# Attention with P times V of key blocks 1, 2 and 3 issued as one group in place of two

## The chip, the cores and the metric

The kernel runs on one core of one Trainium2 chip. The metric is the device time of one execution in microseconds (us); lower is better.

## The reference

One layer of a pre-norm transformer on x of 4 batches, 512 rows and 1024 columns, all in fp32. The attention has 32 query heads of 32 columns, which share one key and one value head. The second half multiplies by a weight of 6-bit codes.

```
q = (hidden_states @ Wq).reshape(b, s, NUM_HEADS, HEAD_DIM)
kv = hidden_states @ Wkv
k, v = (kv[..., :HEAD_DIM], kv[..., HEAD_DIM:])
scores = jnp.einsum('bqhd,bkd->bhqk', q, k) * scale
...
scores = jnp.where(causal[None, None], scores + bias[None], -jnp.inf)
attn = jax.nn.softmax(scores, axis=-1)
out = jnp.einsum('bhqk,bkd->bqhd', attn, v).reshape(b, s, h)
return out @ Wo
...
x = x + _L0_attn_ref(_layernorm(x, axis=-1), L0_attn_Wq, L0_attn_Wkv, L0_attn_Wo)
x = x + _L0_ffn_ref(_layernorm(x, axis=-1), L0_ffn_qweight, L0_ffn_weight_scale, L0_ffn_weight_zero_point, L0_ffn_bias)
```

The change touches only the product of attn and v.

## The kernel before

Four stages follow one another: `project` (layer norm, q, k and v), `attend` (the attention), `split_wo`, and `finish` (output projection and the second half). Only `attend` is changed.

`attend` makes 32 **steps**, one for each batch and group of four heads. Each engine has a program of its own, in the fixed order in which the code issues it; semaphores tie them together. The scores are computed twice. First with queries on the partitions (`score`, tile `p_s`), to find each query's maximum: VectorE (DVE) reduces each block with `maximum`, one column of `mx` for each. Then with keys on the partitions (`score_t`, tile `p_st`), where the maximum enters as two more rows of the contraction; ScalarE (ACT) takes the exponential of it into `pt`, GpSimd (POOL) cuts the diagonal and adds parts for the row totals, and TensorE (PE) multiplies `pt` with V (`values`, tile `p_o`) and with a column of ones (`totals`, tile `p_sum`).

PE's program for step s is a ring of 12 **positions**, 0 to 11. At each stands one `score_t` (at position 5 the transpose `turn_max` in its place), then one or two `score` for a later step (two at positions 0, 3, 6 and 9), and at some positions a group for step s-1, by the tables `VALUES_AT` and `TOTALS_AT`. These say: before, key block 0 at position 1, block 1 at position 4, blocks 2 and 3 at position 6, and the totals at position 9. The scores of one step are named here s0 to s15 as PE issues them: s0 and s1 at position 0, s2 at 1, s3 at 2, s4 and s5 at 3, s6 at 4, s7 at 5, s8 and s9 at 6, s10 at 7, s11 at 8. Their widths are 128, 256, 384 and 512 columns in turn. The maxima on DVE are max0 to max15 in the same order.

The matmuls of `score` and `score_t` are fp32r with 128 stationary columns. Those of `values` and `totals` are fp32 with 32 stationary columns, one for each head in its own quarter of the array (`tile_position`), and four of them, one per head, run at once. `turn_max` is an fp32 transpose of the full array. The trace calls all of these "f32".

How a maximum gets to its use: s3 completes the 16 blocks of the next step, max3 writes the last of them into `mx`, `turn_max` at position 5 waits for it and transposes `mx` into a bank of `p_st`. ACT rounds it (`max_high`, tile `mh`), DVE computes the rest (`max_low`, tile `ml`), and SyncE sends both by DMA into `qst`, where `score_t` at position 0 of the next step reads them. `max_low` is written in DVE's program behind max9 (`if i == 9`). The bank is one of three that `score_t` uses in turn, so `score_t` at position 8, the next user of it, waits for `ml_done` (`free_bank`).

`maximum` waits for the score it reduces; for a block of 128 columns it waits for the next score too (`n + 2 if qb == 0`), since the two share a bank. So max8 waits for s8 and s9.

Of the kernel before, what the change touches and what calls it, by code (L numbers as in the profile page):

```python
# [413 lines left out]
def attend(nc, wo, qh_d, ql_d, ext_d, inv_d, keep, ot, wo_raw):  # L414
# [3 lines left out]
    with ExitStack() as ctx:  # L418
# [84 lines left out]
        def _(pe):  # L503
# [34 lines left out]
            def values(s, kb):  # L538
                b = s // GROUPS
                if kb == 0:  # L540
                    at_least(pe, o_taken, s)
                pe.wait_ge(cut_done, 4 * s + kb + 1)
                for h in range(4):
                    last = pe.matmul(p_o[32 * h:32 * h + 32, kb * P:S], vst[:, TPB * b + kb, :],  # L544
                                     pt[s % 2][:, h, PT_AT[kb]:PT_AT[kb] + KB_LEN[kb]], start=(kb == 0), stop=(kb == 3),
                                     tile_position=(0, 32 * h), skip_group_check=True)
                if kb == 3:
                    last.then_inc(v_done, 1)
# [11 lines left out]
                if part == 1:  # L560
                    last.then_inc(pv_done, 1)

            VALUES_AT = {1: (0,), 4: (1,), 6: (2, 3)}
            TOTALS_AT = {9: (0, 1)}

            def step(s):
                n = 4 * (4 * s + AHEAD)
                for at in range(RING):
# [8 lines left out]
                    if s > 0:  # L577
                        for kb in VALUES_AT.get(at, ()):
                            values(s - 1, kb)
# [483 lines left out]
```

## Time and profile before

| | us |
|---|---|
| median of 3 runs | 979.53 |
| lowest and highest | 978.84 and 981.4 |
| the profiled execution | 978.43 |
| its span, first to last instruction | 976.7 |

The 32 steps of `attend` take some 300 of the 976.7 us, from about 280 to 600. The profile's timeline gives for each instruction its start and its duration in us, and in square brackets how long its engine sat idle before it and which engine ended that. A matmul's duration is modelled and overlaps with that of the next; what a matmul costs is the distance from its start to the next start. PE is the matmul, PEld is the weight load. Rows of `values` are counted x8 for four matmuls of one width, x16 for eight.

### The profile page before, as it was taken

What the parts mean: (1) busy time and instruction counts of PE and PEld (TensorE: products, weight loads), DVE (VectorE), ACT (ScalarE), POOL (GpSimd) and SP (SyncE); (2) the same over time, 40 slices, a digit from 0 to 9 for tenths busy, and PEclk for the clock granted to TensorE, in tenths of its full rate; (3) what the DMA queues carried; (4) which work ended last, traced back from release to release, by engine and by line L of the source; (5) the groups of instructions that cost most, each with busy time, mean ns of one, the idle gap of its engine ahead of it and who ended that gap; (6) DMA issues with size and microseconds to landing.
All of it is one profiled execution on the core that took longest, in us unless ns stands there. A gap on an engine that the chain in (4) does not pass through costs nothing. (4 is left out here: it accounts for less than half of the span.)

```text
span 976.7 us, 13682 instructions
## 1 busy us (share of the span) xinstructions
PE 871.9 (89%) x4912; PEld 633.4 (65%) x4912; DVE 528.9 (54%) x1466; ACT 335.0 (34%) x639; POOL 404.6 (41%) x270
## 2 busy tenths in 40 slices
PE   3689999999488999999999996069999999999996
PEld 2578888888354555555555552047888778887885
DVE  6454352611185777877787781413545564556444
ACT  3222121221034666666666664321111211121111
POOL 1100000000015888888888887134533453335410
PEclk9899999999857999999999998578999999999999
DMA  4533545434574343443334310460242224222311
GB/s 145 193 116 117 187 137 176 147 103 124 135 238 86 80 91 82 90 93 89 84 87 95 86 36 12 147 207 22 73 119 68 65 65 120 74 65 65 104 47 43
DMA packets 63675, 100.52 MB, mean 103 GB/s; under 512 B 6132, under 2 KB 31732, under 8 KB 63544
## 3 DMA queue, kind: packets, MB, share of 16 engines
q1 hardware_dynamic: 61944, 93.62, 35.1%
q0 software_dynamic: 1664, 6.03, 2.0%
q8 instruction: 39, 0.64, 0.3%
q14 instruction: 28, 0.23, 0.1%
HBM read 68.56 MB, written 30.54 MB: 101 GB/s over the span
## 5 line engine op out<-in xcount | busy, mean ns | idle before, releaser
L675 DVE CUSTOM_DVE_ANT_0 spill<-p_s,mask 128x128 bf16<-128x128 f32 (+3 forms) x512 | 224.3, 486 | 89.2 <-PE p_s L512 87.3
L608 ACT ACTIVATE pt<-p_st 128x512 f32<-128x512 f32 (+1 forms) x352 | 179.7, 562 | 98.6 <-PE p_st L535 92.8
L512 PE MATMUL p_s<-kst,qst 98*128 98x128 f32 (+3 forms) x512 | 154.9, 349 | 13.1 <-DMA qst<-ext_d 13.0
L535 PE MATMUL p_st<-qst,kst 100*128 100x512 f32 (+1 forms) x352 | 147.7, 424 | 7.3 <-DMA qst<-ml 6.6
L512 PEld LDWEIGHTS p_s<-kst,qst 98*128 98x128 f32 x512 | 104.0, 206 | 27.6 <-issue 13.5
L828 PE MATMUL p_wo<-woh,osh 128*128 128x512 f32 x256 | 82.7, 405 | 39.4 <-POOL osl L908 37.9
L647 POOL TENSOR_TENSOR pt<-pt 128x1536 f32<-128x1536 f32 x32 | 111.7, 3490 | 2.7
L640 POOL TENSOR_SCALAR_AFFINE_SELECT pt<-pt 128x512 f32<-128x512 f32 x128 | 80.3, 642 | 76.6 <-ACT pt L608 76.6
L908 POOL TENSOR_TENSOR osl<-ot,osh 128x1024 fp32r<-128x1024 f32 x16 | 38.5, 2404 | 171.6 <-ACT osh L868 171.6
L217 PE MATMUL p_q<-xth,wqh 128*128 128x512 f32 x256 | 103.5, 404 | 4.4 <-DVE wql L392 4.4
L535 PEld LDWEIGHTS p_st<-qst,kst 100*128 100x128 f32 x352 | 68.4, 195 | 60.1 <-ACT pt L608 27.1
L217 PE MATMUL p_q<-xtl,wqh 128*128 128x512 f32 x256 | 101.2, 395 | 0.0
L217 PE MATMUL p_q<-xth,wql 128*128 128x512 f32 x256 | 101.1, 395 | 0.0
L949 DVE TENSOR_TENSOR xr<-xr,p_wo 128x1024 f32<-128x1024 f32 x16 | 19.5, 1221 | 137.5 <-PE p_wo L828 137.5
L544 PE MATMUL p_o<-pt,vst 128*32 128x512 f32 (+3 forms) x1024 | 89.6, 445 | 1.7 <-POOL pt L640 1.7
L656 POOL MEMSET mx<- 128x128 f32 x2 | 0.3, 199 | 215.6 <-POOLq L68 215.6
L873 ACT ACTIVATE mv<-mv,eps 128x1 f32<-128x1 f32 x16 | 4.7, 295 | 229.3 <-DVE mv L955 229.3
L838 PE MATMUL p_ff<-wi,yth 128*128 128x512 f32 x256 | 79.8, 393 | 2.9 <-DVE ytl L966 2.9
L828 PEld LDWEIGHTS p_wo<-woh,osh 128*128 128x128 f32 x256 | 48.1, 193 | 52.8 <-POOL osl L908 41.7
L828 PE MATMUL p_wo<-wol,osh 128*128 128x512 f32 x256 | 80.4, 396 | 0.0
L828 PE MATMUL p_wo<-woh,osl 128*128 128x512 f32 x256 | 80.2, 395 | 0.0
L838 PE MATMUL p_ff<-wi,ytl 128*128 128x512 f32 x256 | 79.8, 393 | 0.0
(99 smaller groups left out, 1264.4 us busy)
## 6 DMA issues: line engine op xcount, KB each, us to landing
qst<-qh_d SPq DMA_DIRECT2D x64, 256.0 KB
xin<-in_x_dram SPq DMA_DIRECT2D x16, 512.0 KB, 3.9
qh_d<-qh SPq DMA_DIRECT2D x32, 256.0 KB, 2.6
ql_d<-ql SPq DMA_DIRECT2D x32, 256.0 KB, 3.2
qst<-ql_d SPq DMA_DIRECT2D x32, 256.0 KB
inv_b<-inv_d SPq DMA_DIRECT2D x64, 128.0 KB, 4.8
xr<-in_x_dram SPq DMA_DIRECT2D x16, 512.0 KB, 4.2
out_dram<-ot SPq DMA_DIRECT2D x16, 512.0 KB, 5.2
```

What stands on the lines that cost most here:

```text
L217: last = pe.matmul(out, w[:, c, cols], xt[:, bass.ds(at + c, 1), :].rearrange("p a s -> p (a s)"), start=(c == 0 and k == 0), stop=(c == C ...
L512: pe.matmul(scores_of(n), qst[s % 4][0:R_MAX, j, qb * P:(qb + 1) * P], kst[0:R_MAX, b * S:b * S + keys], start=True, stop=True).then_inc(s ...
L535: pe.matmul(p_st[:, place(k) % 3, 0:heads * KB_LEN[kb]], kst[0:R_END, b * S + kb * P:b * S + (kb + 1) * P], qst[s % 4][0:R_END, j:j + head ...
L544: last = pe.matmul(p_o[32 * h:32 * h + 32, kb * P:S], vst[:, TPB * b + kb, :], pt[s % 2][:, h, PT_AT[kb]:PT_AT[kb] + KB_LEN[kb]], start=(k ...
L608: act.activation(pt[s % 2][:, j:j + heads, PT_AT[kb]:PT_AT[kb] + KB_LEN[kb]], p_st[:, place(k) % 3, 0:heads * KB_LEN[kb]].rearrange("p (j ...
L640: pool.affine_select(out=own, in_=own, compare_op=ALU.is_ge, fill=0.0, base=0, pattern=[[0, 4], [1, P]], channel_multiplier=-1).then_inc(c ...
L647: pool.tensor_tensor(x[:, :, ADD_AT:ADD_AT + 3 * P], x[:, :, PT_AT[0] + P:PT_AT[0] + S], x[:, :, PT_AT[1]:PT_AT[1] + 3 * P], ALU.add).then ...
L675: dve.tensor_tensor_reduce(spill[:, SPILL_AT[qb]:SPILL_AT[qb] + keys], scores_of(n), mask[:, S - keys:S], 1.0, LOWEST, ALU.add, ALU.max, m ...
L828: last = pe.matmul(p_wo[:, n, :], a[:, c, :], w[:, c, n * S:(n + 1) * S], start=(c == 0 and k == 0), stop=(c == CK - 1 and k == 2))
L838: last = pe.matmul(p_ff[:, n, :], a[:, c, :], wi[:, c, n * S:(n + 1) * S], start=(c == 0 and a is yth), stop=(c == CK - 1 and a is ytl))
L908: pool.tensor_tensor(osl[:, :, :].rearrange("p c q -> p (c q)"), o_tile(t), osh[:, :, :].rearrange("p c q -> p (c q)"), ALU.subtract).then ...
L949: dve.tensor_tensor(xt, xt, flat(p_wo[:, :, :]), ALU.add).then_inc(x2_done, 1)
```

## The change

The table of positions is changed. Block 1 moves from position 4 to position 5, behind the transpose and s7; blocks 2 and 3 move from position 6 to position 5, ahead of that position's end. The three then stand behind one another. Nothing is added or taken out.

```
-            VALUES_AT = {1: (0,), 4: (1,), 6: (2, 3)}
+            VALUES_AT = {1: (0,), 5: (1, 2, 3)}
```

The order of PE's program changes, in 31 of the 32 steps (in step 0 there is no earlier step to multiply). The programs of DVE, ACT, POOL and SyncE are the same before and after. The last step's own products stand behind the ring and are not changed.

PE before, from position 4 to the `score_t` of position 8 (`p_st<-qst,kst` is `score_t`, `p_s<-kst,qst` is `score`, `p_st<-ident,mx` is the transpose, `32x384` and the like are `values`):

```order
L535 MATMUL p_st<-qst,kst 128x384
L512 MATMUL p_s<-kst,qst 128x384
L544 MATMUL p_o<-pt,vst 32x384 x4
L527 MATMUL p_st<-ident,mx 128x128
L512 MATMUL p_s<-kst,qst 128x512
L535 MATMUL p_st<-qst,kst 128x384
L512 MATMUL p_s<-kst,qst 128x128
L512 MATMUL p_s<-kst,qst 128x256
L544 MATMUL p_o<-pt,vst 32x256 x4
L544 MATMUL p_o<-pt,vst 32x128 x4
L535 MATMUL p_st<-qst,kst 128x384
L512 MATMUL p_s<-kst,qst 128x384
```

PE after, the same place:

```order
L535 MATMUL p_st<-qst,kst 128x384
L512 MATMUL p_s<-kst,qst 128x384
L527 MATMUL p_st<-ident,mx 128x128
L512 MATMUL p_s<-kst,qst 128x512
L544 MATMUL p_o<-pt,vst 32x384 x4
L544 MATMUL p_o<-pt,vst 32x256 x4
L544 MATMUL p_o<-pt,vst 32x128 x4
L535 MATMUL p_st<-qst,kst 128x384
L512 MATMUL p_s<-kst,qst 128x128
L512 MATMUL p_s<-kst,qst 128x256
L535 MATMUL p_st<-qst,kst 128x384
L512 MATMUL p_s<-kst,qst 128x384
```

Two things moved: the transpose has no `values` ahead of it any more, and s8 and s9 (128 and 256 columns) now stand behind all of blocks 1, 2 and 3, where they stood ahead of blocks 2 and 3. The next instruction behind each excerpt is the `score_t` of position 8.

## Rows read from the trace of the kernel before

**Rows 1.** Head of the page: the span and the busy time of each engine.
```profile
span 976.7 us, 13682 instructions
PE 871.9 (89%) x4912; PEld 633.4 (65%) x4912; DVE 528.9 (54%) x1466; ACT 335.0 (34%) x639; POOL 404.6 (41%) x270
```

**Rows 2.** Busy time by stretch: start and end, length, then each engine, granted clock last.
```profile
320.75:330.50 9.75, 9.75 (x78) 5.63 (x77) 7.22 (x36) 6.33 (x14) 8.25 (x7) 1.00 0.38 86
330.50:505.72 175.22, 175.22 (x1369) 101.17 (x1369) 135.57 (x604) 114.80 (x237) 148.50 (x109) 1.00 0.39 87
620.00:976.00 356.00, 316.33 (x1408) 258.88 (x1408) 167.25 (x179) 58.28 (x97) 131.58 (x53) 0.95 0.30 88
```

**Rows 3.** Timeline of PE, an inner step, from block 0 to position 8.
```profile
320.75 1.06 PE L544 MATMUL p_o<-pt,vst 128*32 128x512 f32 x8
321.75 0.50 PE L535 MATMUL p_st<-qst,kst 100*128 100x512 f32 x1
322.09 0.40 PE L512 MATMUL p_s<-kst,qst 98*128 98x512 f32 x1
322.32 0.40 PE L535 MATMUL p_st<-qst,kst 100*128 100x512 f32 x1
...
322.98 0.33 PE L512 MATMUL p_s<-kst,qst 98*128 98x384 f32 x1
323.25 0.85 PE L544 MATMUL p_o<-pt,vst 128*32 128x384 f32 x8
324.03 0.33 PE L527 MATMUL p_st<-ident,mx 128*128 128x128 f32 x1
324.12 0.48 PE L512 MATMUL p_s<-kst,qst 98*128 98x512 f32 x1
324.43 0.34 PE L535 MATMUL p_st<-qst,kst 100*128 100x384 f32 x1
324.61 0.39 PE L512 MATMUL p_s<-kst,qst 98*128 98x128 f32 x2
324.93 0.86 PE L544 MATMUL p_o<-pt,vst 128*32 128x256 f32 x16
325.72 0.44 PE L535 MATMUL p_st<-qst,kst 100*128 100x384 f32 x1
326.00 0.33 PE L512 MATMUL p_s<-kst,qst 98*128 98x384 f32 x1
326.24 0.44 PE L535 MATMUL p_st<-qst,kst 100*128 100x384 f32 x1
```

**Rows 4.** Timeline of the same step: max3, POOL's addition, ml, position 8.
```profile
322.63 0.69 DVE L675 CUSTOM_DVE_ANT_0 spill<-p_s,mask 128x512 bf16<-128x512 f32 x1 [0.82 <-PE p_s L512]
...
322.90 2.38 POOL L653 TENSOR_TENSOR pt<-pt 128x1024 f32<-128x1024 f32 x1
...
323.25 0.08 DVE L675 DVE_READ_ACCUMULATOR2_ANT mx<- 128x1 f32 x1
...
325.92 0.27 DVE L682 SCALAR_TENSOR_TENSOR ml<-p_st,mh 16x128 fp32r<-16x128 f32 x1
...
326.24 0.19 PEld L535 LDWEIGHTS p_st<-qst,kst 100*128 100x128 f32 x1 [0.22 <-DVE ml L682]
```

**Rows 5.** Timeline of step 0, which has no values groups, positions 6 to 8.
```profile
285.73 0.63 PE L512 MATMUL p_s<-kst,qst 98*128 98x128 f32 x2
...
286.50 0.29 DVE L675 CUSTOM_DVE_ANT_0 spill<-p_s,mask 128x128 bf16<-128x128 f32 x1
...
286.72 0.42 DVE L675 CUSTOM_DVE_ANT_0 spill<-p_s,mask 128x256 bf16<-128x256 f32 x1
...
287.06 0.27 DVE L682 SCALAR_TENSOR_TENSOR ml<-p_st,mh 16x128 fp32r<-16x128 f32 x1
...
287.39 0.69 PE L535 MATMUL p_st<-qst,kst 100*128 100x384 f32 x1 [0.40 <-DVE ml L682]
```

**Rows 6.** Timeline of POOL near the end of the stage, step 30.
```profile
589.80 3.48 POOL L647 TENSOR_TENSOR pt<-pt 128x1536 f32<-128x1536 f32 x1
```

## The prediction

> **What bounds the kernel now.** I read the head of the page first, then the busy time by stretch, then the timeline of one inner step. The head shows PE busy for 89% of the span, the next engine 54% [rows 1]. The stretches show that inner steps are alike: 320.75 to 330.50 is one step, and 330.50 to 505.72 is 18 steps in 175.22 us, 9.73 us each. In both PE is busy all the time at a granted clock of 1.00 (2.4 GHz), while DVE has 7.2 of 9.75 us, ACT 6.3 and POOL 8.25 [rows 2]. So the step lasts as long as PE needs for its list, plus whatever PE waits. The timeline shows how near such waits are. At position 8, the weight load was released by ml on DVE: ml starts at 325.92, lasts 0.27, ends at 326.19, and PE goes on at 326.24 [rows 3, 4]. s10, of 384 columns, starts at 326.00; the `score_t` of 384 columns at 324.43 is followed by the next start after 0.18, so PE was ready for position 8 at 326.18 [rows 3]. It lost 0.06 us. This chain (s9, max9, ml, position 8) has no slack before the change; the total shares of busy time don't tell this.
>
> **What a group costs beside its columns.** Block 0, 512 columns, takes 321.75 - 320.75 = 1.00 us; block 1, 384 columns, 324.03 - 323.25 = 0.78; blocks 2 and 3, together 384 columns, 325.72 - 324.93 = 0.79 [rows 3]. So 128 columns cost 0.22, blocks behind one another add nothing, and a group has a fixed part of about 1.00 - 4 x 0.22 = 0.12 to 0.15 us. Further, the last score ahead of a group takes longer (322.98 to 323.25 is 0.27 against 0.18, so 0.08 to 0.09 for the entry), and the first `score_t` behind one also (325.72 to 326.00 is 0.28 against 0.18, 0.10 for a weight load that isn't hidden) [rows 3]. One group fewer saves some 0.15 + 0.08 + 0.10 = 0.33 us a step. But before, the transpose rode directly behind block 1, in place of that `score_t`: T to s7 is 0.09 and s7 to the next is 0.31, against 0.23 for a 512-column score such as 322.09 to 322.32 [rows 3]. It needs these 0.40 us wherever it stands.
>
> The Trainium skill (TensorEngine Tiling (Array Packing), Key Properties) says that a change of tiling mode drains TensorE. The rows' 0.12 to 0.15 of fixed cost agrees with that. Going by the rule alone, one switch to quarter-array tiles and back is dropped in each step, nothing is added, and the kernel gets faster; that is rival A below.
>
> **The new step, instruction by instruction.** I lay the changed list on the clock of the inner step, which runs unchanged up to s6 at 322.98.
> - PE is ready for the transpose at 322.98 + 0.18 = 323.16. The transpose needs max3: it starts at 322.63, its last read of the accumulator is 323.25 + 0.08 = 323.33 [rows 4], and a release takes PE about 0.05 (ml end 326.19, PE 326.24). So the transpose starts at 323.39: a new wait of 0.23. Before, block 1 covered it, and nothing showed.
> - s7 at 323.39 + 0.09 = 323.48. Behind it the group can start after 0.31 + 0.08: 323.87. No row shows a transpose, one score and a group in a row; 0.31 is what s7 takes before, and the least is 0.23, so the start lies between 323.71 and 323.87. I take the later, as 0.31 is from the same pair.
> - The group has 768 columns: 1.00 + 2 x 0.22 = 1.44, so position 6 starts at 325.31.
> - Position 6: its `score_t` pays the unhidden load, 0.28, so s8 and s9 start at 325.59, 0.98 us later than the 324.61 of before [rows 3].
> - PE would then be ready for position 8 after 0.24 + 0.18 + 0.18 (a pair of 384 columns without a group behind it, a `score_t` of 384, s10): 326.19. That is 0.05 ahead of the 326.24 of before. So far the change is worth about nothing: the transpose's wait and its own mode change eat the saving.
> - But max8 waits for s8 and s9, and ml stands behind max9. Duration of the pair 0.39, end 325.98. DVE starts 0.14 behind a score's end (322.09 + 0.40 = 322.49, max3 at 322.63). max8 to max9 takes 0.22, max9 to ml 0.34, ml 0.27, release 0.06 [rows 3 to 5]. Sum 325.98 + 0.14 + 0.22 + 0.34 + 0.27 + 0.06 = 327.01.
> - Position 8 starts at 327.01 in place of 326.24: **+0.77 us** a step, of which PE waits 0.82 for ml.
>
> Step 0 shows this very order, since it has no groups: s8 and s9 at 285.73, max8 at 286.50, ml at 287.06, position 8 at 287.39 with a wait put down to ml [rows 5]. From the pair's end (285.73 + 0.63 = 286.36) that is 1.03 us; my sum above has the same 1.03.
>
> **What follows position 8.** From there all four engines keep their distance to PE. ml ends just ahead of position 8 before and after, so its DMA to `qst`, needed at position 0 of the next step, has the same time. POOL's cut of block 1 follows the exponential of position 8, and has 1.5 us of idle in a step (9.75 - 8.25, [rows 2]); it shifts with PE. Blocks 2 and 3 are wanted 0.4 us earlier (324.93 before; 323.87 plus 0.66 for block 1 is 324.53) and were cut by 322.90, where POOL turned to its next addition [rows 4]. The copy of `p_o` and the totals come later in the step, when their inputs are there. Nothing makes the 0.77 good: a later reduction on DVE finds its score ready earlier, but PE waits for none of them.
>
> **The sum.** Steps 2 to 29 have the whole list: 28 x 0.77 = 21.6 us. Step 1 starts at 1.2 GHz; there its matmuls cover the wait for max3, which leaves 0.77 - 0.23 = about 0.5. Step 30 has no s8 and s9, so ml isn't held; but its position 6 gets later by what blocks 1 to 3 ahead of it cost, less what the merged group saves, some 0.6 us, and POOL's chain, whose addition at 589.80 leads to the last totals, starts from the exponential of position 8 [rows 6]: +0.6 as an estimate. Step 31 waits for POOL: 0. Sum 21.6 + 0.5 + 0.6 = 22.7. The profiled execution took 978.43 us with a span of 976.7 [rows 1], so 1001.1; the median of the runs is 979.53, 1.1 above it, and would give 1002.2. I predict 1001.5.
>
> Bounds of a step: if the group starts at 323.71 and the transpose's release comes 0.1 sooner, 0.77 - 0.26 = 0.5, so 28 x 0.5 + 1 = +15. If s8 to position 7 pay a further unhidden load of 0.10 each, for which the rows behind a long group speak, 0.95: +28. That is 993 to 1007.
>
> **Rivals.**
> - *A: the merged group's saving comes through.* One switch of tiles fewer, as said. Its place is position 8: it decides for "faster" if DVE has ml out before PE is ready. If only the wait for ml vanished, a step gains 0.05 and the time is 978, no change. If the transpose's wait of 0.23 vanished too, a step gains 0.28: 29 x 0.28 = 8 us, 971. For it speaks that DVE has 2.5 us of idle in a step [rows 2]. Against it, that idle is exactly the time in which DVE has no score to reduce, and the order of DVE's program doesn't change. 0.06 for both, half of it for 978.
> - *B: the wait is only half as long,* since PE's durations are modelled and the pair's true end or the reduction's start may come sooner: 0.4 us a step, 28 x 0.4 + 1 = 12 us, 991. Step 0's measured 1.03 speaks against it. 0.08.
> - *C: the clock falls.* PE now stands still for 0.23 + 0.82 of 10.5 us. In the last stage, where PE is busy 316 of 356 us, the mean granted clock was 0.95 [rows 2], so part of it ran at 1.2 GHz. If `attend` had 0.95 as well, its 300 us would be 5% longer on top: 1001 + 15 = 1016. Each wait is far below 1 us, and the inner steps are 90% busy. 0.06.
> - The change does what it says: the order of PE's program has the three blocks behind one another.
>
> **How the numbers follow.** My forecast has 0.80, A 0.06, B 0.08, C 0.06. The likeliest gives 1001.5. The bounds of the unknown costs give 993 to 1007; A, B and C lie outside and hold 0.20. A measurement of this kernel can tell about 0.3% (3 us) from no change. Faster by over 0.3% is half of A, 0.03; within it the other half, 0.03; slower all the rest, 0.94.
>
> **What would show it.** In the profile after: the inner step is 10.5 us long; PE's weight load at L535 waits for ml on DVE by 0.8 us once a step, some 24 us in all; the transpose's load waits for mx on DVE with no group ahead of it, so that PE itself stands for 0.2; values at L544 in one run of 1.44 us; s8 to max8 to ml to position 8 in 1.42 us. PE's busy share in `attend` falls from 100% to about 90%. I am wrong if ml is out before PE is at position 8, or if the transpose starts at once and s8 comes 0.3 us sooner than said, or if the granted clock leaves 1.00 in inner steps.

## The result: 1002.9 us, 2.4% slower

| kernel | median us | ratio to before, 95% interval |
|---|---|---|
| before | 979.66 | |
| after | 1002.88 | 1.0236 [1.0216, 1.0255] |

The forecast was 1001.5 us, in a range of 993 to 1007. The profiled execution of after has a span of 1000.8 us against 976.7, so 24.1 more. Its page, beside [rows 1]: PE did the same work (872.0 us busy against 871.9) in a longer span. What is new is the idle time: `score_t` matmuls, which had no wait for ml among their largest before, now waited 20.4 us for it.

```profile
span 1000.8 us, 13682 instructions
PE 872.0 (87%) x4912; PEld 634.1 (63%) x4912; DVE 526.4 (53%) x1466; ACT 332.6 (33%) x639; POOL 404.7 (40%) x270
...
L535 PE MATMUL p_st<-qst,kst 100*128 100x512 f32 (+1 forms) x352 | 148.1, 425 | 27.8 <-DVE ml L682 20.4
```

The timeline of PE, an inner step, from its position 2 on. It answers to [rows 3], where position 2 starts at 321.75; add 1.14 to a time there to have it here.

```profile
322.89 0.50 PE L535 MATMUL p_st<-qst,kst 100*128 100x512 f32 x1
...
324.12 0.33 PE L512 MATMUL p_s<-kst,qst 98*128 98x384 f32 x1
324.53 0.33 PE L527 MATMUL p_st<-ident,mx 128*128 128x128 f32 x1
324.61 0.47 PE L512 MATMUL p_s<-kst,qst 98*128 98x512 f32 x1
325.01 1.50 PE L544 MATMUL p_o<-pt,vst 128*32 128x384 f32 x24
326.45 0.44 PE L535 MATMUL p_st<-qst,kst 100*128 100x384 f32 x1
326.73 0.40 PE L512 MATMUL p_s<-kst,qst 98*128 98x128 f32 x2
326.96 0.34 PE L535 MATMUL p_st<-qst,kst 100*128 100x384 f32 x1
327.14 0.34 PE L512 MATMUL p_s<-kst,qst 98*128 98x384 f32 x1
328.16 0.45 PE L535 MATMUL p_st<-qst,kst 100*128 100x384 f32 x1 [0.69 <-DVE ml L682]
```

The transpose stands behind no group any more, and its load waits for max3; s6 to the transpose is 0.41 (324.12 to 324.53) where 0.18 would do:

```profile
324.52 0.14 PEld L527 LDWEIGHTS p_st<-ident,mx 128*128 128x128 f32 x1 [0.40 <-DVE mx L675]
```

And the row on DVE, from the same stretch, that PE waits for, with max8 ahead of it. It answers to [rows 4]:

```profile
327.27 0.29 DVE L675 CUSTOM_DVE_ANT_0 spill<-p_s,mask 128x128 bf16<-128x128 f32 x1 [1.16 <-PE p_s L512]
...
327.83 0.27 DVE L682 SCALAR_TENSOR_TENSOR ml<-p_st,mh 16x128 fp32r<-16x128 f32 x1
```

What to see: s10 starts at 327.14 and position 8 at 328.16, 1.02 us later; a score of 384 columns with nothing to wait for takes 0.18. So PE lost 0.84 us here. (The profile says 0.69, since it counts from the modelled end of s10.) DVE in turn had been idle for 1.16 us, from 326.11 to 327.27: max7 was done 0.34 before the group's end at 326.45, and the next scores, s8 and s9, came only behind the `score_t` of position 6. The two engines waited for each other in turn. The step lasts 10.53 us against 9.73. The stretch by engine, to be read beside [rows 2], has the granted clock at 1.00:

```profile
322.89:333.42 10.53, 9.77 (x80) 5.66 (x76) 7.11 (x35) 6.24 (x13) 8.24 (x7) 1.00 0.36 81
```

### The profile page after: what moved, and what is told of

It reads as the page before. It is cut to its first block and busy times, and to the rows that moved or that the text cites. A ratio compares the mean times of both kernels' runs of the same rounds, so it can differ in the third digit from the quotient of the medians.

```text
span 1000.8 us, 13682 instructions
## 1 busy us (share of the span) xinstructions
PE 872.0 (87%) x4912; PEld 634.1 (63%) x4912; DVE 526.4 (53%) x1466; ACT 332.6 (33%) x639; POOL 404.7 (40%) x270
## 5 line engine op out<-in xcount | busy, mean ns | idle before, releaser
L608 ACT ACTIVATE pt<-p_st 128x512 f32<-128x512 f32 (+1 forms) x352 | 177.3, 561 | 143.6 <-PE p_st L535 143.0
L535 PE MATMUL p_st<-qst,kst 100*128 100x512 f32 (+1 forms) x352 | 148.1, 425 | 27.8 <-DVE ml L682 20.4
L512 PE MATMUL p_s<-kst,qst 98*128 98x128 f32 (+3 forms) x512 | 154.9, 350 | 13.5 <-DMA qst<-ext_d 13.4
L535 PEld LDWEIGHTS p_st<-qst,kst 100*128 100x128 f32 x352 | 68.3, 195 | 83.4 <-DVE ml L682 30.1
L512 PEld LDWEIGHTS p_s<-kst,qst 98*128 98x128 f32 x512 | 104.0, 206 | 26.9 <-issue 13.9
L544 PE MATMUL p_o<-pt,vst 128*32 128x512 f32 (+3 forms) x1024 | 83.2, 442 | 1.7 <-POOL pt L640 1.7
```

The source lines that it names most:

```text
L512: pe.matmul(scores_of(n), qst[s % 4][0:R_MAX, j, qb * P:(qb + 1) * P], kst[0:R_MAX, b * S:b * S + keys], start=True, stop=True).then_inc(s ...
L535: pe.matmul(p_st[:, place(k) % 3, 0:heads * KB_LEN[kb]], kst[0:R_END, b * S + kb * P:b * S + (kb + 1) * P], qst[s % 4][0:R_END, j:j + head ...
L608: act.activation(pt[s % 2][:, j:j + heads, PT_AT[kb]:PT_AT[kb] + KB_LEN[kb]], p_st[:, place(k) % 3, 0:heads * KB_LEN[kb]].rearrange("p (j ...
```

## The experiments

All times are medians; "inner step" is the distance between two transposes in the profile. In this order the kernels first show where the loss is, then what a group costs, then where a merge could pay.

| run | merged | ml behind | inner step us | median us | ratio, 95% interval |
|---|---|---|---|---|---|
| before | no | max9 | 9.73 | 979.7 | |
| after | 1-3 at position 5 | max9 | 10.53 | 1002.9 | 1.0236 [1.0216, 1.0255] |
| e1 | 1-3 at 5 | max7 | 9.69 | 978.4 | 0.9993 [0.9977, 1.0009] |
| e9 | 1-3 at 5 | max8 | 10.19 | 992.2 | 1.0131 [1.0098, 1.0164] |
| e2 | 1-3 at 5 | max10 | 11.01 | 1025.3 | 1.0462 [1.0436, 1.0488] |
| e4 | 1-3 at 6 | max9 | 9.67 | 977.5 | 0.9979 [0.9966, 0.9993] |
| e3 | no | max7 | 9.58 | 974.3 | 0.9944 [0.9927, 0.9962] |
| e5 | no, 1 at 5, 2-3 at 6 | max9 | 9.91 | 985.4 | 1.0056 [1.0035, 1.0077] |
| e6 | 1-3 at 6, transpose too | max9 | 9.66 | 978.5 | 0.9983 [0.9973, 0.9994] |
| e11 | 1-3 at 4 | max7 | 9.82 | 982.9 | 1.0033 [1.0019, 1.0046] |
| e7 | 0 with totals | max9 | 9.62, some 10.40 | 985.3 | 1.0056 [1.0039, 1.0074] |
| e8 | 0 with totals | max7 | 9.45, some 10.23 | 979.4 | 1.0006 [0.9993, 1.0018] |
| e10 | as e8, reciprocal moved | max7 | 9.45 | 970.0 | 0.9899 [0.9878, 0.9920] |

### Is it ml? Moving it on DVE alone: e1, e9, e2

The theory is that the whole loss is the distance from s9 to ml. The rival is that the long group itself costs. The edit is on DVE alone; PE's order stays that of after.

```
-                    if i == 9 and s + 1 < STEPS:
+                    if i == 7 and s + 1 < STEPS:
                         max_low(s + 1)
```

> The changed kernel with max_low two reductions earlier on VectorE (behind max7 in place of max9); TensorE's order stays the merged one. Theory: ml no longer waits for s8 and s9, is out about 0.8 us before TensorE is at position 8, and the step falls from 10.53 to 9.69 us (9.74 less the 0.05 by which TensorE is ready sooner): 978.5 us, the wait of p_st for ml gone, the transpose's wait of about 0.2 still there. Rival (the long run of fp32 matmuls itself starves ScalarE and VectorE, or costs more than its columns): the time stays at 1000 or more whatever ml does.

978.4 us and 9.69 us a step: both as the theory says. The loss is gone with the merged group in place. The rows of PE at positions 7 and 8, with no wait; the second row is position 8, 0.17 us behind s10:

```profile
325.13 0.34 PE L512 MATMUL p_s<-kst,qst 98*128 98x384 f32 x1
325.30 0.34 PE L535 MATMUL p_st<-qst,kst 100*128 100x384 f32 x1
...
325.95 0.30 PEld L512 LDWEIGHTS p_s<-kst,qst 98*128 98x128 f32 x2 [0.28 <-DVE mx L675]
```

The third row is a wait that is left. The scores at position 9 go into the bank of s8 and s9 and so wait for max9, which is late here for the same reason as ml was: its score stands behind the long group. It costs 0.10 us (325.72 to 326.38 is 0.66, and 0.56 in e3 below).

The same edit with `i == 8`:

> The changed kernel with max_low behind max8, between the 10.53 us step of the changed kernel and the 9.69 with ml behind max7. Theory: ml is out 0.34 us earlier, and position 8 with it: step 10.19 us, 29 x 0.34 = 10 us under 1002.9, 993 us, with the granted clock at 1.00 in all inner steps.

992.2 us, 10.19 us a step, as expected. And with `i == 10`:

> The changed kernel with max_low one reduction later (behind max10, 384 columns, 0.48 us from start to start). Theory: if the whole loss is the distance from s9 to ml, the step grows by the same 0.48: 29 x 0.48 = 14 us on 1002.9, 1017 us. Rival (the long group is what costs): ml has slack or is second in line, and 1003 to 1006.

The step grew by 0.48 to 11.01 us, as the theory says, but the time by 22 us where 14 were expected. In the profile, five steps took 1.6 us more than the others: the totals of these five last over 2.2 us in place of 1.28. One of the five and the step ahead of it, by stretch:

```profile
356.05:367.05 11.00, 9.77 (x78) 5.66 (x77) 7.12 (x36) 6.25 (x14) 8.26 (x7) 1.00 0.32 75
367.05:379.65 12.60, 11.37 (x78) 6.32 (x77) 7.21 (x36) 6.43 (x15) 9.86 (x9) 0.86 0.30 67
```

The granted clock is 0.86 in the long one, so for part of it PE had 1.2 in place of 2.4 GHz. The totals are the first to be slow, 1.06 us behind the end of the step's longest wait; the matmuls in between keep their usual distances. The full clock was back within the same step:

```profile
373.81 0.44 PE L535 MATMUL p_st<-qst,kst 100*128 100x384 f32 x1 [1.16 <-DVE ml L682]
...
374.87 2.33 PE L557 MATMUL p_sum<-pt,pick 128*32 128x512 f32 x16
```

29 x 0.48 = 14 and 5 x 1.6 = 8 make 22 us. The medians are 22.4 apart, the two profiled executions 20.4. The other three runs of e2 were 1.9 to 3.7 us longer than the profiled one, at a mean clock of 0.935 to 0.938 against 0.944, so they may have had more such steps; they left no trace to show it. In after no inner step's totals were that slow. The two kernels differ only in the place of ml, so what rival C of the prediction names does happen in this kernel when PE's wait is made longer: with 1.3 us (from start to start, beyond s10's own 0.18) in five of the steps, with the 0.84 of after in none.

### The same merge behind s8 and s9: e4

```
-            VALUES_AT = {1: (0,), 5: (1, 2, 3)}
+            VALUES_AT = {1: (0,), 6: (1, 2, 3)}
```

> Blocks 1, 2 and 3 in one group, but at position 6, behind s8 and s9; max_low stays behind max9. Theory: the group now covers max8, max9 and ml, as blocks 2 and 3 did before; step 9.69 us, 978.5 us. Rival (three groups in place of four are slower by themselves, by a longer idle time of ScalarE or VectorE): 1000 or more.

977.5 us, 9.67 us a step. DVE's program is that of after. Position 6's `score_t` and its two scores, s8 and s9, moved from behind the group to ahead of it, and the 25 us are gone. Together with e1, where only ml moved, this shows the cause from both sides.

### What ml cost before the change: e3

The kernel before with `i == 7`.

> The kernel before with max_low behind max7. Theory: only the 0.06 us that position 8 waited for ml is won, 29 x 0.06 = 1.7 us, so 978 us, no change that can be told. If ml were a bottleneck of the kernel before by more than that, the time would fall by 5 us or more.

974.3 us: 5.5 us faster, three times what I expected. The step went from 9.73 to 9.58. PE at positions 7, 8 and s11, to be read beside the last rows of [rows 3]:

```profile
326.37 0.34 PE L512 MATMUL p_s<-kst,qst 98*128 98x384 f32 x1
326.38 0.19 PEld L535 LDWEIGHTS p_st<-qst,kst 100*128 100x128 f32 x1
326.55 0.34 PE L535 MATMUL p_st<-qst,kst 100*128 100x384 f32 x1
326.73 0.39 PE L512 MATMUL p_s<-kst,qst 98*128 98x512 f32 x1
```

s10 to position 8 is 0.18 (0.24 before), and position 8 to s11 is 0.18 too, where it was 0.28. A wait of 0.06 cost 0.16. The load row tells why: without the wait, the weights of position 8 are loaded from 326.38, 0.17 us ahead of their matmul and under s10; before, load and matmul both start at 326.24, behind ml, so part of the load of 0.19 us is no longer hidden, 0.10 by the distance to s11. I had counted the 0.10 behind a group and not behind a wait. That makes 29 x 0.15 = 4.4 of the 5.5 us; the rest is no more than what single runs differ by.

### What one group costs: e5

```
-            VALUES_AT = {1: (0,), 5: (1, 2, 3)}
+            VALUES_AT = {1: (0,), 5: (1,), 6: (2, 3)}
```

> Block 1 at position 5 behind the transpose and s7, blocks 2 and 3 at position 6: the transpose is uncovered as in the changed kernel, but there are four groups, and s8 and s9 stand ahead of the last. Theory: by the rows, position 8 starts 0.26 us later than before (a group's fixed cost of 0.33 comes back, less the 0.06 of the ml wait): step 10.0 us, 29 x 0.26 = 7.5, 987 us. The difference to the merged group at position 6 is the price of one more group: 0.31 a step, 9 us. If a group switch costs nothing, both are equal at 978.

985.4 us, 9.91 us a step. Against e4 one group more costs 9.91 - 9.67 = 0.24 us, 29 x 0.24 = 7 of the measured 7.9 us. By the rows I had 0.31; in e4, s8 has to wait for a maximum (`PEld p_s L512 <- DVE mx`), which gives 0.05 back. By the rows it is then 0.29, near the 0.31. So merging groups does save what it should. The Trainium skill (TensorEngine Tiling (Array Packing), Key Properties) has a change of tiling mode drain TensorE; this pair of runs agrees with that. It can't tell such a drain from the weight load behind the group, which is in the same 0.24.

### Can the wait for max3 be avoided? e6 and e11

In e4 the transpose still waits 0.23 us. e6 sets `TURN_AT = 6` on top of e4, so that the transpose stands behind one more `score_t` and s7.

> The merged group at position 6 and the transpose of the maxima at position 6 too, one score_t and s7 later than before, so that it doesn't wait for max3; max_low stays behind max9, position 9 is the next user of its bank. Theory: against the merged group at position 6 the transpose's wait of 0.23 goes: step 9.4 us, about 970 us, faster than both kernels. Rivals: the transpose comes too late for mh, ml and their DMA to position 0 of the next step (3.2 us), which then waits, and the time stays at 978; or VectorE or ScalarE fall behind without a group in positions 2 to 5.

978.5 us, 9.66 us a step: nothing gained, where I had expected 970. The wait had moved to s7, and s8 now waits as well:

```profile
324.13 0.19 PEld L512 LDWEIGHTS p_s<-kst,qst 98*128 98x128 f32 x1 [0.21 <-DVE mx L675]
324.13 0.51 PE L512 MATMUL p_s<-kst,qst 98*128 98x512 f32 x1
324.48 0.27 PE L527 MATMUL p_st<-ident,mx 128*128 128x128 f32 x1
324.69 0.30 PEld L512 LDWEIGHTS p_s<-kst,qst 98*128 98x128 f32 x2 [0.28 <-DVE mx L675]
```

s7 writes the bank of `p_s` that s3 had, and so waits for max3 as well; s8 waits in the same way for max5, which comes behind max3. The one `score_t` now ahead of s7 covers 0.17 us of this; before the change, block 1 with its 0.78 covered it all. From s6 to the group PE needs 1.39 us, as in e4. Neither the theory nor the rivals named this. e11 puts the group there, on top of e1:

```
-            VALUES_AT = {1: (0,), 5: (1, 2, 3)}
+            VALUES_AT = {1: (0,), 4: (1, 2, 3)}
```

> Blocks 1, 2 and 3 in one group at position 4, ahead of the transpose and s7 (which both need max3), with max_low behind max7. The group now covers max3, but the transpose comes 0.65 us later than before. Theory, from the rows: max7 ends 0.62 us after its start at s7's end + 0.14, ml 0.33 behind that, position 8 at 326.35 on the clock of the inner step against 326.08 with the early ml alone; step 9.58 + 0.27 = 9.85 us, 982 us. Rival: the full saving of a merge shows (0.33 under 9.58), 965 us.

982.9 us, 9.82 us a step, as expected. The transpose no longer waits, but it comes later, and ml with it; position 8 waits again (`[0.33 <-DVE ml L682]` in 27 of the steps). A single long group, at position 4, 5 or 6, never covered both max3 and the chain to ml; the two groups of before did, but for 0.06 us.

### A merge elsewhere: e7, e8, e10

Block 0 of a step can follow the totals at position 9 of the same step, in place of position 1 of the next. The edit is shown against the kernel before. (Block 0 of the last step, which stood behind the ring, moves as well.)

```
-            VALUES_AT = {1: (0,), 4: (1,), 6: (2, 3)}
+            VALUES_AT = {4: (1,), 6: (2, 3)}
...
                         for part in TOTALS_AT.get(at, ()):
                             totals(s - 1, part)
+                    if at == 9:
+                        values(s, 0)
```

> The kernel before with another pair of groups merged: block 0 of a step directly behind the totals at position 9 of the same step, in place of position 1 of the next; blocks 1 to 3, the transpose and s8 and s9 stay. Theory: a merge that leaves everything ahead of max3 and ml in place keeps its saving of 0.33 us (0.15 fixed, 0.08 entry, 0.10 weight load): step 9.40 us, 29 x 0.33 = 9.7, 970 us. Rival (merging never pays, since what feeds TensorE has no slack: VectorE and ScalarE now see seven positions without a group and TensorE waits for them): 978 or more.

985.3 us: slower, my expectation missed by 15. Most steps took 9.62 us in place of 9.40, and twelve took 0.8 more (10.40 to 10.48, and 9.86 for the last, which has fewer scores). e8 has the early ml on top:

> The same, with max_low behind max7. Theory: both gains add, 0.33 and the 0.155 measured for the early ml: step 9.25 us, 965 us, faster than all others. Rival: the two overlap, and it equals the one without the early ml.

979.4 us, 14 above what I expected, with steps of 9.45 and twelve that took 0.8 more, mostly 10.23. The twelve are those in which DVE makes a reciprocal of the row totals. In one of them:

```profile
407.29 0.95 DVE L691 RECIPROCAL inv<-sums 128x128 f32<-128x128 f32 x1
...
408.88 0.48 PE L512 MATMUL p_s<-kst,qst 98*128 98x128 f32 x2 [0.72 <-DVE mx L677]
```

Positions 10 to 4 now follow each other without a group. There DVE needs more time for its maxima than PE for the scores, and PE waits for banks: 0.2 us in the other steps, and 0.8 more where the reciprocal of 0.95 us falls in the same stretch. Ahead of it, behind the long group, DVE is idle for up to 1.82 us. e10 moves the reciprocal there:

```
-                if s > GROUPS and s % GROUPS in (2, 3, 4, 5):
-                    invert(s // GROUPS - 1, s % GROUPS - 2)
+                    if i == 13 and s > GROUPS and s % GROUPS in (2, 3, 4, 5):
+                        invert(s // GROUPS - 1, s % GROUPS - 2)
```

> The kernel with block 0 behind the totals and ml behind max7, and each reciprocal of the row totals moved on VectorE from behind max15 to behind max13, where VectorE stands idle for 1.8 us behind the long group. In the run without this, the 12 steps with a reciprocal lasted 10.23 us and the others 9.43 to 9.47. Theory: the merge had used up VectorE's slack in positions 10 to 4, and the reciprocal (0.95 us) came on top; moved, all steps are 9.45: 12 x 0.78 = 9.4 less than 979.4, 970 us. Rival: the reciprocal delays the next maxima there too, and the steps stay at 10.2.

970.0 us, with about 9.45 us in the steps of either kind, 1.0% faster than before. The next maximum behind a reciprocal still found DVE idle, for 0.96 us:

```profile
402.24 0.95 DVE L691 RECIPROCAL inv<-sums 128x128 f32<-128x128 f32 x1
...
404.14 0.56 DVE L677 CUSTOM_DVE_ANT_0 spill<-p_s,mask 128x384 bf16<-128x384 f32 x1 [0.96 <-PE p_s L512]
```

e10 beats both kernels. It has three groups a step, like the changed kernel, but keeps blocks 1 and 2-3 where they cover max3 and ml. Of the 9.4 us that it gains, 5.5 come with the early ml alone (e3). The other 4.3, against e3, are the merge's: 29 x (9.58 - 9.45) = 3.8, the saving of a group less the 0.2 that PE waits for banks. No kernel has the reciprocal moved without this merge, but in e3 the steps with a reciprocal took 9.58 like the others (two took 9.62 and 9.80), so it had next to nothing to gain there.

## Why the prediction was right, point by point

- **The chain at position 8** was right, and was the whole matter. From position 2 to position 8 the step was laid out as 327.01 - 321.75 = 5.26 us; measured, 328.16 - 322.89 = 5.27. Each link agrees within 0.02: transpose 1.64 behind position 2, group 0.48 behind the transpose, 1.44 for the group, 0.28 to the pair, 0.54 to max8, 0.56 to ml, 0.33 to position 8. e1, e9, e2 and e4 show that it is the cause and not only beside it.
- **The sum.** The step grew by 0.80, not 0.77: 28 x 0.80 = 22.4 in place of 21.6. Step 30 was estimated at +0.6: its block 0 starts 23.23 us later than before (606.83 against 583.60), and POOL's addition in it 23.87 (613.67 against 589.80, [rows 6]), so 0.64. What is left of the 24.1 us of span, about 1, is step 1 (0.56, estimated at 0.5) and two single steps that were longer: one of 10.88, in which the transpose waited 0.35 longer for max3, and one of 10.67, in which a load waited 0.36 for the DMA of ml.
- **The wait's size in the views.** I said that the weight load would wait 0.8 a step. The load's own idle time is 1.00 and the matmul's 0.69; the loss is neither but the distance from start to start, 0.84. Over the whole run the load waits 30.1 us for ml and the matmul 20.4, where I had said 24. PE was busy for 9.77 of 10.53 us, 93%, where I had said about 90.
- **"So far the change is worth about nothing"**: e1 has ml out of the way and is at 978.4, the same as before within its interval. Up to position 8 the working holds: e1 needs 4.44 us from position 2 to position 8 (320.86 to 325.30), before 4.49. Behind it luck helped, as two terms that I had at nothing cancelled: s11 comes 0.10 sooner, since position 8 no longer stands behind a wait (e3), and the totals come 0.10 later, since the scores at position 9 wait for max9. Measured from e3, which has no wait for ml at all, the merge at position 5 loses 0.11 a step even with ml early: from s6 to s11 a group fewer and the transpose's wait are even (3.39 against 3.37 us), and the wait for max9 is the rest. In after itself neither of the two terms changed anything, since position 8 stands behind a wait before and after, and max9 is done before it.
- **Rival A** was worked out wrongly in its second half: that a step gains 0.28 if the transpose's wait goes. s7 waits for max3 too (e6), and moving the transpose behind it gained nothing. Its place was position 8 indeed, and there it fell.
- **Rival B** (half the wait) fell: max8 started 0.14 behind the end of its scores (326.73 + 0.40 to 327.27), as in step 0 (286.36 to 286.50, [rows 5]).
- **Rival C** (the clock) didn't happen here: 1.00 from 311 to 600 us. But the reason that I gave, that each wait is far below 1 us, doesn't fit a wait of 0.82, and e2 shows the clock falling 0.5 us of wait further on. The 0.06 was low for so small a distance.
- Not foreseen in the prediction, and shown by e7 and e8: DVE's 2.5 us of idle time a step are no slack. Where a merge takes a group out of a stretch, DVE becomes the bound of that stretch.

## What to carry to other kernels

A group of matmuls that looks like mere overhead may be the cover of a wait on another engine. Before merging, list what every engine's next operation needs and which group runs meanwhile; an engine that is busy 100% of the time only says that every wait is covered, not by how much. When an order is moved on one engine, move what stands in the queue of the other with it: one number on VectorE gave back the 24 us, and another merge, with two things moved on VectorE, made the kernel 1% faster, over half of it by the early ml alone.

## What the runs showed of the hardware

- A wait on a semaphore costs more than its length: 0.06 us of waiting for ml cost 0.16, since the weight load of 0.19 us behind it, which otherwise starts 0.17 us ahead of its matmul, was no longer wholly hidden (e3).
- The granted clock fell to 1.2 GHz for parts of five steps in e2's profile. Each fall showed first in the totals, some 1.1 us behind the end of a wait of 1.3 us or a little more, and cost 1.6 us. The steps around these have waits of the same length and stayed at 1.00, and so did all inner steps of after, with waits of 0.84 us.
- Groups of quarter-array fp32 matmuls behind one another cost nothing extra: 768 columns took 1.44 us, 1.00 + 2 x 0.22. One more separate group cost 0.24 us (e5 against e4), 0.29 without e4's own wait of 0.05.
- The end of a matmul, as modelled, to the start of the DVE instruction that waits for it is 0.14 us (327.13 to 327.27), and the end of a DVE instruction to the load on PE that waits for it 0.06 (328.10 to 328.16).
